# Layer norms in a vision-text block: the scaling of rows done by ScalarE instead of VectorE

## The reference

```
tokens = patches(14x14 of 16x16x3) @ W.T + b         # 196 rows an image
h  = concat([class_token, tokens] + pos_embed, txt)  # 197 + 128 = 325 rows an image
y1 = (h - mean(h)) / sqrt(var(h) + 1e-5)             # layer norm over the 192 columns
q, k, v = split(y1 @ W_qkv + b_qkv)
h  = h + ((q @ k.T) / sqrt(192) * decay_mask) @ v    # no softmax; mask 0.99**(i-j), lower triangle
y2 = layernorm(h)
sig = sigmoid(y2 @ Wg.T);  the 6 best of 128 experts by sig + e_bias, weights 2.5 * sig / sum
h  = h + routed experts (at most 192 tokens each, silu(g) * u, width 464) + shared expert (width 928)
```

## Time and profile before

| | us |
|---|---|
| median of 3 runs | 805.89 (803.89 to 806.28) |
| the profiled execution's own time | 812.84 |
| its span | 811.2 |
| busy: TensorE, VectorE, ScalarE, GpSimd | 722.8, 513.1, 280.6, 187.4 |

### The profile page before, as it was taken

How to read it: one execution, slowest core, us unless ns; L and a number is a source line. 1 busy time by engine, 2 the same in 40 slices (tenths; PEclk the granted TensorE clock), 3 DMA queues, 4 the chain that set the end, 5 groups by cost and what they waited for, 6 DMA issues and landing times.

```text
span 811.2 us, 16672 instructions
## 1 busy us (share of the span) xinstructions
PE 722.8 (89%) x4729; PEld 676.2 (83%) x4730; DVE 513.1 (63%) x1655; ACT 280.6 (35%) x645; POOL 187.4 (23%) x245
## 2 busy tenths in 40 slices
PE   2799999999999828899898999998989998989894
PEld 2799889998999727789898989898989898979883
DVE  1468988888888874545646565656564646465641
ACT  0233323322333323434434343334343434343421
POOL 2121111111111001200323232323232323232330
PEclk9799999999999958899999999899999999898997
DMA  5336334333432524231435353535353535353521
GB/s 157 101 96 210 110 116 133 106 123 119 132 104 91 157 70 110 67 62 16 85 78 107 83 100 84 99 84 99 84 99 84 100 83 100 81 102 78 105 46 22
DMA packets 75138, 78.75 MB, mean 97 GB/s; under 512 B 6529, under 2 KB 66891, under 8 KB 75116
## 3 DMA queue, kind: packets, MB, share of 16 engines
q1 hardware_dynamic: 63004, 65.98, 30.0%
q0 software_dynamic: 12112, 12.50, 10.3%
HBM read 51.15 MB, written 19.32 MB: 87 GB/s over the span
## 4 chain that ended last, share of the span: by engine, by line
PE 37%; DMA 13%; issue 5%; DVE 3%; DVEq 1%; POOL 1%; ACT 1%; POOLq 0%
PE bank L1221 16%; DMA x_rows<-yw_rows,get_idx 11%; PE bank L1236 6%; PE bank L1203 5%; PE bank L1191 4%; PE bank L1237 3%; PE bank L1165 1%; DMA result<-y_rows,put_idx 1%; DVE s_inter L1428 1%; PE bank L1240 1%; DVEq L911 1%; DMA result<-s_rows 1%; PE bank L1172 1%; POOL x_rows L1004 1%; PE bank L1173 0%
## 5 line engine op out<-in xcount | busy, mean ns | idle before, releaser
L1428 DVE TENSOR_TENSOR s_inter<-s_gate,bank 128x384 f32<-128x384 f32 (+1 forms) x112 | 60.4, 540 | 83.0 <-PE bank L1221 71.7
L1236 PE MATMUL bank<-s_dn,s_in_hi 128*128 128x384 f32 (+1 forms) x287 | 101.1, 409 | 1.2 <-DVE s_in_lo L1436 1.2
L1065 ACT ACTIVATE s_gate<-bank 128x384 f32<-128x384 f32 (+1 forms) x112 | 53.7, 480 | 84.7 <-PE bank L1221 84.7
L499 PE MATMUL bank<-w_tok,patches 128*128 128x192 f32 x384 | 70.4, 343 | 9.1 <-DMA patches<-xp 9.1
L1237 PE MATMUL bank<-s_dn,s_in_lo 128*128 128x192 f32 (+1 forms) x287 | 78.3, 273 | 0.0
L1221 PE MATMUL bank<-all_hiA,s_hi 128*128 (+4 forms) x210 | 74.4, 354 | 3.1 <-DVE y_rows L1415 1.6
L499 PEld LDWEIGHTS bank<-w_tok,patches 128*128 128x128 f32 x384 | 66.5, 201 | 9.1 <-issue 7.5
L1221 PE MATMUL bank<-all_B,s_lo 128*128 (+4 forms) x210 | 70.9, 338 | 0.0
L1221 PE MATMUL bank<-all_B,s_hi 128*128 (+4 forms) x210 | 70.9, 337 | 0.0
L1221 PE MATMUL bank<-all_loA,s_hi 128*128 (+4 forms) x210 | 70.8, 337 | 0.0
L1221 PE MATMUL bank<-all_hiA,s_lo 128*128 (+4 forms) x210 | 70.8, 337 | 0.0
(11 more groups left out here) (178 smaller groups left out, 1877.8 us busy)
## 6 DMA issues: line engine op xcount, KB each, us to landing
raw_gu<-wgu SPq DMA_DIRECT2D x22, 464.0 KB, 5.3
raw_gu<-wgu SPq DMA_DIRECT2D x44, 232.0 KB, 6.7
patches<-xp SPq DMA_DIRECT2D x16, 588.0 KB, 4.5
down_w<-wdn SPq DMA_DIRECT2D x22, 348.0 KB
result<-s_rows POOLq DMA_DIRECT2D x13, 288.0 KB, 4.9
result<-h SPq DMA_DIRECT2D x16, 192.0 KB
yw_rows<-y SPq DMA_DIRECT2D x16, 192.0 KB
all_hiA<-y_hiA SPq DMA_DIRECT2D x16, 162.5 KB, 2.1
```

The source lines that it names most:

```text
L499: mm = pe.matmul(tok_ps[:, t * D:(t + 1) * D], patches[:, c, t * 128:(t + 1) * 128], w_tok[:, c, :], start=c == 0, stop=c == KC - 1)
L1065: act.activation(s_gate[m % 2][0:r, 0:width], up_banks(m, alone)[0][0:r, 0:width], ACT.Silu).then_inc(s_gate_ready, 1)
L1236: pe.matmul(bank[0:r, 0:2 * D], s_in_hi[:, m, rows], s_dn[:, m, :], start=m == 0, stop=False)
L1428: dve.tensor_tensor(s_inter[m % 2][0:r, 0:width], s_gate[m % 2][0:r, 0:width], up, ALU.mult).then_inc(s_inter_ready, 1)
```

## The change

`normed` leaves VectorE's program and enters ScalarE's. There a tile is one activation, y = rstd * h + shift with rstd and shift per row. GpSimd makes shift = -mean * rstd in two more operations: the negated mean (`below`, in front of the power) and the product (`shift`, behind it, with a wait on a new semaphore `s_pow`). In ScalarE's step y2(n) stands between the split of y1T(n+1) and the copies of q and k, y1(n+2) between the counts and the split of y2T(n); in its prologue y1(0) stands behind the set-up copies, and y1(1) ahead of the copies of q and k of image 0. VectorE's residual waits for the last y2, since ScalarE now reads `h1`. ScalarE's wait for GpSimd's memsets moves ahead of that for the constants.

```diff
--- before.py
+++ after.py
@@ -184,10 +184,10 @@
         for i, y in ((1, y1), (2, y2)):
             norm.append(dict(
                 y=y, stats=sb(f"stats{i}", [128, 3, 6]), mv=sb(f"mv{i}", [128, 3, 2]), ve=sb(f"ve{i}", [128, 3]),
-                rstd=sb(f"rstd{i}", [128, 3]), hiA=sb(f"y{i}_hiA", [128, SP], F32R),
+                rstd=sb(f"rstd{i}", [128, 3]), below=sb(f"below{i}", [128, 3]), shift=sb(f"shift{i}", [128, 3]), hiA=sb(f"y{i}_hiA", [128, SP], F32R),
                 loA=sb(f"y{i}_loA", [128, SP], F32R), st=sb(f"y{i}_B", [128, SP], F32R),
                 s_stats=sem(f"stats{i}_done"), s_mv=sem(f"mv{i}_ready"), s_ve=sem(f"ve{i}_ready"),
-                s_rstd=sem(f"rstd{i}_ready"), s_y=sem(f"y{i}_ready"), s_T=sem(f"y{i}T_in_psum"),
+                s_pow=sem(f"pow{i}_ready"), s_rstd=sem(f"rstd{i}_ready"), s_y=sem(f"y{i}_ready"), s_T=sem(f"y{i}T_in_psum"),
                 s_hi=sem(f"y{i}T_hi_ready"), s_lo=sem(f"y{i}T_split"), bankA=psum[5 if i == 1 else 3],
                 bankB=psum[6 if i == 1 else 4]))
         n1, n2 = norm
@@ -362,10 +362,12 @@
             def rstd_pool(pool, c, n):
 
                 wait_apart(pool, passed, (c["s_mv"], n + 1))
-                pool.tensor_scalar(c["ve"][:, :], c["mv"][:, :, 1], EPS, None, ALU.add).then_inc(c["s_ve"], 1)
-                pool.wait_ge(c["s_ve"], n + 1)
-                wait(pool, c["s_y"], n)
-                pool.tensor_tensor(c["rstd"][:, :], c["ve"][:, :], half_neg[:, :], ALU.pow).then_inc(c["s_rstd"], 1)
+                pool.tensor_scalar(c["ve"][:, :], c["mv"][:, :, 1], EPS, None, ALU.add)
+                pool.tensor_scalar(c["below"][:, :], c["mv"][:, :, 0], -1.0, None, ALU.mult).then_inc(c["s_ve"], 1)
+                wait_apart(pool, passed, (c["s_ve"], n + 1), (c["s_y"], n))
+                pool.tensor_tensor(c["rstd"][:, :], c["ve"][:, :], half_neg[:, :], ALU.pow).then_inc(c["s_pow"], 1)
+                wait_apart(pool, passed, (c["s_pow"], n + 1))
+                pool.tensor_tensor(c["shift"][:, :], c["below"][:, :], c["rstd"][:, :], ALU.mult).then_inc(c["s_rstd"], 1)
 
             @block.gpsimd
             def _(pool):
@@ -410,6 +412,7 @@
 
             @block.scalar
             def _(act):
+                act.wait_ge(pool_set, 2)
                 act.wait_ge(const_in, 16 * N_CONST)
                 act.activation(qkv_hi[:, :, :], raw_qkv[:, :, :], ACT.Copy).then_inc(set_up_act, 1)
                 act.activation(g_hi[:, :, :], raw_g[:, :, :], ACT.Copy).then_inc(set_up_act, 1)
@@ -423,6 +426,17 @@
                     act.activation(c["hiA"][:, 0:S], c["bankA"][:, 0:S], ACT.Copy)
                     act.activation(c["st"][0:DB, 0:S], c["bankB"][0:DB, 0:S], ACT.Copy).then_inc(c["s_hi"], 1)
 
+                def normed(c, h, n):
+                    act.wait_ge(c["s_rstd"], n + 1)
+                    wait(act, c["s_T"], n)
+                    if c is n2:
+                        wait(act, y_out, 32 * n)
+                    for t in range(3):
+                        r = TL[t]
+                        ins = act.activation(c["y"][0:r, t, 0:D], h[0:r, t, :], ACT.Identity,
+                                             bias=c["shift"][0:r, t:t + 1], scale=c["rstd"][0:r, t:t + 1])
+                    ins.then_inc(c["s_y"], 1)
+
                 def qk_evac(n):
                     wait(act, sc_mm, 3 * n)
                     for m in range(4):
@@ -453,16 +467,22 @@
                         sigmoid(n - 1)
                     if more:
                         split_hi(n1, n + 1, v_mm, 1)
+                    normed(n2, h1, n)
+                    if more:
                         qk_evac(n + 1)
                     if behind:
                         counts(n - 1)
+                    if not isinstance(n, int) or n < B - 2:
+                        normed(n1, h0[:, by_turns(n + 2), :], n + 2)
                     split_hi(n2, n, lg_mm, 1)
 
                 def shared_hi(half):
                     act.wait_ge(s_in, 48 + 96 * half)
                     act.activation(s_hi[:, half, :], raw_s[:, :], ACT.Copy).then_inc(s_hi_set, 1)
 
+                normed(n1, h0[:, by_turns(0), :], 0)
                 split_hi(n1, 0, v_mm, 1)
+                normed(n1, h0[:, by_turns(1), :], 1)
                 qk_evac(0)
                 step(0)
                 step(1)
@@ -628,17 +648,6 @@
                         ins = dve.bn_aggr(c["mv"][0:TL[t], t, :], c["stats"][0:TL[t], t, :])
                     ins.then_inc(c["s_mv"], 1)
 
-                def normed(c, h, n):
-                    dve.wait_ge(c["s_rstd"], n + 1)
-                    wait(dve, c["s_T"], n)
-                    if c is n2:
-                        wait(dve, y_out, 32 * n)
-                    for t in range(3):
-                        r = TL[t]
-                        ins = dve.tensor_scalar(c["y"][0:r, t, 0:D], h[0:r, t, :], c["mv"][0:r, t, 0:1],
-                                                c["rstd"][0:r, t:t + 1], ALU.subtract, ALU.mult)
-                    ins.then_inc(c["s_y"], 1)
-
                 def split_lo(c, n):
                     dve.wait_ge(c["s_hi"], n + 1)
                     dve.tensor_tensor(c["loA"][:, 0:S], c["bankA"][:, 0:S], c["hiA"][:, 0:S].bitcast(F32), ALU.subtract)
@@ -657,6 +666,7 @@
                 def residual(n):
                     dve.wait_ge(pv_mm, n + 1)
                     wait(dve, h1_out, 32 * n)
+                    wait(dve, n2["s_y"], n)
                     dve.tensor_tensor(h1[:, 0:2, :], pv_ps[:, 0:2 * D].rearrange("p (t c) -> p t c", t=2),
                                       h0[:, bass.ds((n % 2) * 3, 2), :], ALU.add)
                     dve.tensor_tensor(h1[0:TL[2], 2, :], pv2_ps[0:TL[2], 0:D],
@@ -746,7 +756,6 @@
                         token_rows(n + 2)
                     if behind and more:
                         weights(n - 1)
-                    normed(n2, h1, n)
                     if behind and not more:
                         weights(n - 1)
                     if more:
@@ -754,12 +763,9 @@
                         decay(n + 1)
                     if behind:
                         count_full(n - 1)
-                    if ahead:
-                        normed(n1, h0[:, by_turns(n + 2), :], n + 2)
                     split_lo(n2, n)
 
                 token_rows(0)
-                normed(n1, h0[:, by_turns(0), :], 0)
                 dve.wait_ge(const_in, 16 * N_CONST)
                 dve.wait_ge(set_up_act, 2)
                 dve.tensor_tensor(qkv_lo[:, :, :], raw_qkv[:, :, :], qkv_hi[:, :, :].bitcast(F32),
@@ -769,7 +775,6 @@
                 dve.tensor_copy(cum[:, :, :], cum32[:, :, :]).then_inc(lo_set, 1)
                 split_lo(n1, 0)
                 token_rows(1)
-                normed(n1, h0[:, by_turns(1), :], 1)
                 values(0)
                 decay(0)
                 def shared_lo(half):
```

## The result

| | before | after |
|---|---|---|
| median, us | 805.26 (22 runs, 798.43 to 810.09) | 809.06 (22 runs, 803.7 to 811.23) |
| the profiled execution: own time, span | 812.84, 811.2 | 809.91, 808.2 |
| busy: TensorE, VectorE, ScalarE, GpSimd | 722.8, 513.1, 280.6, 187.4 | 717.6, 487.8, 325.0, 199.6 |

What follows compares the result with a forecast made beforehand. VectorE's queue, not its busy share, was taken to cost time, making TensorE wait about once a step. Loop -7.2, prologue +4.65 and clock +2.4 gave -0.15 us: 805.7 us, range 801.5 to 810.

Steps and rivals of the forecast that it cites:

- Loop: Block A's loop: each step 0.60 us shorter as VectorE's queue delays TensorE less, 12 steps, -7.2 us.
- The forecast's list of steps: Block A's loop: the gain comes in n=2 and n=4 to 14, not in the first two, step 3 or the last.
- ScalarE's price: ScalarE's activations with scale and shift from memory: 0.50 us each, 1.32 for three, hidden in the loop.
- GpSimd: Two small operations at 0.28 us each; shift ready 0.6 us after the old rstd, later being a sign of error.
- Rival (c): Loop: GpSimd makes the shift late, so y1 on ScalarE delays the split of y2T; 811.8 us, chance 0.13.
- pieces 1 and 2: Prologue: late table load, y1(0), and y1(1) ahead of the q and k copies delay image 0's scores, +4.65 us.
- piece 1: Prologue: table load behind the constants and y1(0) on ScalarE delay qkv of image 0, +1.6 us.
- its two cases: Prologue: full clock returns at the same time (qkv 1.3 us later) or 6.0 us after the new start (2.0).
- Piece 3: Prologue into step 0: TensorE's 3.0 us idle brings half clock for 3 to 7 us, +2.4 us (0 to 3.4).
- (a): Rival, prologue: the clock stays up or falls for an instant only; 803.3 us, chance 0.22.
- (b): Rival, loop: both gaps before TensorE's loads go, 0.91 us a step, 10.9 in all; 802.0 us, chance 0.13.
- (d): Rival: longer waits fill VectorE's time, the gain is nil, the prologue still pays; 812.9 us at most, chance 0.07.

Runs made afterwards that it cites:

- 7: Changed kernel with y1(1) behind the q and k copies in ScalarE's prologue, and y2 in the loop back on VectorE; 808.08 us, ratio 1.0029 to before.
- 3: Changed kernel plus nine unused TensorE products between q, k, v and the scores of image 0; 803.91 us, ratio 0.9963 to before.
- 2: Changed kernel with y1(1) moved behind the copies of q and k of image 0 on ScalarE; 798.49 us, ratio 0.9891 to before.
- 12: The changed kernel again, unchanged, one execution for a second trace; 819.02 us.

## Why the prediction was wrong, step by step

- **Loop: right.** 7.33 us gained where 7.2 was forecast; 0.64 and 2.76 us after the turn where 0.6 and 2.74 stood. The forecast's list of steps holds too: by the turns of y2 step 2 gained 0.41 us, step 3 0.01, and steps 4 to 14 about 0.63 each. 7 confirms which wait ends last by its 0.15.
- **ScalarE's price: a little low.** Mean 538 ns of one and 1.42 for three, where 0.50 and 1.32 were taken. The Trainium skill ("ScalarE: Activation LUTs", What ACT_TABLE_LOAD costs) gives 186 ns, 0.833 ns an element and 93 ns for each of two pointer operands, an estimate of 532 ns for this shape, and 1.41 for three with its overlap; the trace agrees with the page. y1 ended 0.12 us ahead of its deadline where 0.5 was forecast, so it was hidden by luck of a tenth.
- **GpSimd: right in kind, too low.** Negation 0.23 to 0.24, product 0.19, each with a gap of 0.2 to 0.3 beside it: y1's shift is there 0.85 us after the old rstd (2.12 us from the start of `ve`, 138.36 to 140.48, against 148.23 - 146.96 = 1.27), not 0.6, and that was named as a sign of being wrong. y1 therefore started behind the shift and not behind the counts (0.30 idle), but still ended in time. Rival (c) is out.
- **Prologue, pieces 1 and 2: right.** Scores at 41.62, forecast 41.5; 4.77 us, forecast 4.65. Within it piece 1 was 1.37 at the first products for q, k and v (33.64 against 32.27), forecast 1.6: the clock came back at 31.1, near the first of its two cases (31.5, and not 6.0 us after the new start).
- **Piece 3: the step that failed.** The fall was forecast, its length wasn't: "half clock of 3 to 7 us costs half of that", +2.4. It lasted 10.2 us and cost 4.6, measured by 3 and by 15.70 against 20.29. Why it lasted that long stays open: TensorE was as busy in it as in the 3.4 us of step 14. My upper end, 3.4, was too low as well. I had one return of the clock to go by, 6.0 us after unbroken work began, and made it nearly the upper end of the range instead of one case.
- **Step 14: not in the sum.** 1.5 us in the profiled execution. I had put such shifts down to block B alone.

With 4.6 in place of 2.4 the forecast's own sum is -7.2 + 4.65 + 4.6 = +2.05, and 2.03 was measured at the turn of y1(15). Rivals (a) and (b) fell with it: the clock didn't stay up, and a step gained 0.63, not 0.91. (d) named the right sign for a wrong reason.

## What to carry to other kernels

An operation that moves to an idle engine enters that engine's queue at one place for the loop and at another for the prologue; read both, and put it behind what TensorE waits for next: one line moved here turned 0.5% slower into 1.1% faster, with more than block A shows. Price an idle stretch of 3 us in front of TensorE not by its length but by its length and the half clock behind it, here 3.3 us and 4.6 more. Of moved work only that counts that stood ahead of the wait that ends last (0.54 and 0.15 us a step for the same three instructions).

## What the runs showed of the hardware that was not expected

- After an idle stretch of 3.3 us TensorE ran at 1.2 GHz for 10.2 us although it was busy (7.68 of 8.00 us), for the same 10.2 us in four traces of four; with the gap filled, in one trace, the clock stayed at 2.4 GHz.
- After an idle stretch of 2.11 us the clock fell in one execution (0.86, then 0.50) and stayed at 1.00 in another of the same program, 1.5 us apart; it fell in 9 of 13 traces, for 3.4 us each time. What sets 3.4 in one place and 10.2 in the other no run shows.
- At the start the full clock came 3.1 to 6.0 us after the first transposes in the eleven traces with y1(0) on ScalarE (2 and 12 at the low end, 3 at the high one). Most of the 1.8 us between the turns of y2(0) in 2 and 7, which have the same prologue, comes from that.
- Block A ended within 1 us in two traces of the kernel before and of the kernel after (305.64 and 305.88; 309.22 and 308.63), while the whole executions lay 11 and 9 us apart. With so much spread in block B, marks inside the trace told more than the times.
